# Token shifts folded into doubled weights in a four-layer kernel on one core

## The reference, cut to what matters

```python
xa = _ln(x, ln1_w, ln1_b)
sx = concat([state[:, 1:2] - xa[:, :1], xa[:, :-1] - xa[:, 1:]], axis=1)   # token shift
xxx = tanh((xa + sx * maa_x) @ maa_w1).reshape(b, l, 5, 32)               # mixing network
xxx = einsum('blfd,fde->blfe', xxx, maa_w2)
xm = xa[:, :, None] + sx[:, :, None] * (maa_stack + xxx)                  # five mixed inputs
...                                                                       # w, r, k, v, g and the scan
og = ((og - m) / sqrt(va + 1e-05)).reshape(b, l, e) * gn_w + gn_b
x1 = x + og * g @ Wo.T
xc = _ln(x1, ln2_w, ln2_b)
sx2 = concat([state[:, 0:1] - xc[:, :1], xc[:, :-1] - xc[:, 1:]], axis=1)  # token shift
rr = sigmoid((xc + sx2 * ffn_maa_r) @ Wfr.T)
kk = square(relu((xc + sx2 * ffn_maa_k) @ Wfk.T))
return x1 + rr * (kk @ Wfv.T)
```

## Time and profile before

| | us |
|---|---|
| median of 3 runs (lowest, highest) | 2241.07 (2231.89, 2241.25) |
| the profiled execution | 2240.95 |
| its span, first to last instruction | 2239.2 |
| TensorE, VectorE busy | 1800.2, 1363.9 |
| ScalarE, GpSimd busy | 849.3, 860.1 |

### The profile page before, as it was taken

How to read it: one execution, slowest core, us unless ns; L and a number is a source line. 1 busy time by engine, 2 the same in 40 slices (tenths; PEclk the granted TensorE clock), 3 DMA queues, 4 the chain that set the end, 5 groups by cost and what they waited for, 6 DMA issues and landing times. The chain is left out here.

```text
span 2239.2 us, 37086 instructions
## 1 busy us (share of the span) xinstructions
PE 1800.2 (80%) x13613; PEld 1098.1 (49%) x13613; DVE 1363.9 (61%) x2332; ACT 849.3 (38%) x1680; POOL 860.1 (38%) x905
## 2 busy tenths in 40 slices
PE   3888887888788787887888878788887888788765
PEld 2565444654356444554445634465444654456413
DVE  3652568635886368753687446873578645875283
ACT  1443432533425333353333533253432543425202
POOL 3531257302672037511384114830257303752060
PEclk9999998999899898898988989899988999889967
DMA  5000011010210102010020101201011010200030
GB/s 157 1 1 25 7 39 39 2 41 1 48 30 13 29 1 63 15 35 7 15 63 1 34 8 25 53 2 41 1 39 39 2 39 1 63 15 11 1 77 10
DMA packets 73611, 61.24 MB, mean 27 GB/s; under 512 B 38960, under 2 KB 56512, under 8 KB 73408
## 3 DMA queue, kind: packets, MB, share of 16 engines
q1 hardware_dynamic: 49600, 41.70, 8.9%
q10 hardware_dynamic: 23264, 16.85, 2.6%
q0 software_dynamic: 544, 0.03, 0.0%
HBM read 20.28 MB, written 4.19 MB: 11 GB/s over the span
## 5 line engine op out<-in xcount | busy, mean ns | idle before, releaser
L1508 POOL TENSOR_TENSOR soft_ring<-soft_ring,seg_max 128x512 f32<-128x512 f32 x256 | 324.2, 1274 | 471.7 <-DVE seg_max L1349 470.9
L1056 ACT ACTIVATE soft_ring<-soft_ring 128x512 f32<-128x512 f32 x256 | 160.8, 628 | 399.3 <-POOL soft_ring L1508 391.6
L658 PE MATMUL bank<-late,pick 128*128 128x512 f32 x256 | 176.4, 779 | 97.4 <-DVE late L1197 97.1
L1343 DVE SCALAR_TENSOR_TENSOR soft_ring<-bank,mask 128x512 f32<-128x512 f32 x256 | 164.4, 683 | 108.2 <-PE bank L716 100.4
L1470 POOL TENSOR_TENSOR late<-late 128x520 f32<-128x520 f32 x128 | 188.7, 1474 | 64.8 <-DMA late<-late 50.1
L1185 DVE TENSOR_TENSOR_SCAN late<-late 128x520 f32<-128x520 f32 x128 | 188.3, 1471 | 19.2 <-POOL late L1472 13.7
L857 PEld LDWEIGHTS bank<-ident,soft_ring 128*128 128x128 f32 x1024 | 126.5, 151 | 122.8 <-issue 97.8
L857 PE MATMUL bank<-ident,soft_ring 128*128 128x128 f32 x1024 | 170.0, 298 | 19.8 <-ACTq L1067 14.0
L1516 POOL TENSOR_SCALAR soft_ring<-soft_ring,rden 128x256 f32<-128x256 f32 x64 | 59.1, 924 | 312.4 <-DVE rden L1310 312.4
L716 PE MATMUL bank<-early 64*128 64x512 f32 (+1 forms) x512 | 128.2, 603 | 58.6 <-ACTq L1049 55.2
L1349 DVE TENSOR_REDUCE seg_max<-soft_ring 128x8 f32<-128x512 f32 (+1 forms) x256 | 169.3, 676 | 8.9 <-DVE early L1406 1.9
(11 more groups left out here) (242 smaller groups left out, 3430.1 us busy)
## 6 DMA issues: line engine op xcount, KB each, us to landing
late<-late SPq DMA_DIRECT2D x128, 260.0 KB, 3.0
c<-in_ctx ACTq DMA_DIRECT2D x8, 512.0 KB, 4.3
x<-in_x ACTq DMA_DIRECT2D x8, 512.0 KB, 5.9
out_x<-late SPq DMA_DIRECT2D x8, 512.0 KB, 5.0
mask<-in_mask_Bx1xSxS_ff ACTq DMA_DIRECT2D x16, 128.0 KB, 4.6
w<-in_L_xattn_mlp_w ACTq DMA_DIRECT2D x2, 1024.0 KB
mask<-in_mask_BxS_ik SPq DMA_DIRECT2D x8, 256.0 KB, 4.1
wkv<-in_L_xattn_kv_w ACTq DMA_DIRECT2D x1, 512.0 KB
```

The costliest lines, as they stand in the source:

```text
L658: mm(t[:, :], pick[:, j, :], rs[:, j % 2, :], start=j == 0, stop=j == HS - 1).then_inc(full if j == HS - 1 else sig("rs_used"), 1)
L1056: af(soft[:, u % SOFT, :], soft[:, u % SOFT, :], ACT.Exp).then_inc(sig("exp"), 1)
L1343: stt(out=cuts(u, soft[:, u % SOFT, :]), in0=cuts(u, t[:, :]), scalar=HD1 ** -0.5 if u < UNITS else 1.0 / HD2, in1=mask.unsqueeze(1).broad ...
L1508: tt(s, s, seg_max[:, u % SOFT, 0:segs].unsqueeze(2).broadcast_to([128, segs, 512 // segs]), ALU.subtract).then_inc(sig("sub"), 1)
```

## The change

Both token shifts are written as sums: (x + (prev - x) * m) @ W = x @ (W - mW) + prev @ (mW), with mW the weights scaled row by row. The setup makes `wback` (for `Wfk` and `Wfr`) and `maa1_back`, the scaled weights, and subtracts them from the originals. "maa", "ffn k" and "ffn r" then run twice as many products, on `xcP` or `xaP` at offset 1 and 0. "shift 2" leaves the list of stages, with its entry in `PACE`, so that "ffn k", "ffn r" and "ffn v" fall on steps 58, 60 and 62 (`i` = 54, 56 and 58). "shift" makes `sx` alone. "ffn r" splits its token tile into two halves of 64. `maa2` shrinks to two slabs without zeros, and the mix products contract over 32 rows. The gate uses two operations in place of three. The setup's weight copies wait for their own end.

```diff
-        maa2 = sb("maa2", [128, NMIX, E])
+        maa2 = sb("maa2", [128, 2, E])
...
+        maa1_back = sb("maa1_back", [128, KT, NMIX * DM])
+        wback = {w: sb(f"b_{w}", [128, KT, E]) for w in ("Wfk", "Wfr")}
...
-                for t in (maa2, td2, vbd, pick, ones2):
+                for t in (td2, vbd, pick, ones2):
...
-                    nc.vector.tensor_copy(wt[w][:, :, :].rearrange("p k n -> p (k n)"), t[:, :]).then_inc(free, 1)
+                    link(nc.vector.tensor_copy(wt[w][:, :, :].rearrange("p k n -> p (k n)"), t[:, :]))
+                    dve.sem_inc(free, 1)
...
+                for w, f in (("Wfk", "ffn_k"), ("Wfr", "ffn_r")):
+                    for k in range(KT):
+                        ins = nc.vector.tensor_scalar(wback[w][:, k, :], wt[w][:, k, :], v(f, k), None, ALU.mult)
+                for k in range(KT):
+                    ins = nc.vector.tensor_scalar(maa1_back[:, k, :], maa1[:, k, :], v("maa_x", k), None, ALU.mult)
+                link(ins)
+                nc.vector.tensor_tensor(maa1[:, :, :], maa1[:, :, :], maa1_back[:, :, :], ALU.subtract)
+                for w in wback:
+                    nc.vector.tensor_tensor(wt[w][:, :, :], wt[w][:, :, :], wback[w][:, :, :], ALU.subtract)
...
-                  ["center", "variance", "gate", "project", "moments 2", "normalize 2", "turn 2", "shift 2", "ffn k", "ffn r", "ffn v"])
+                  ["center", "variance", "gate", "project", "moments 2", "normalize 2", "turn 2", "ffn k", "ffn r", "ffn v"])
...
-        PACE = {"r u k": 2.2, "shift": 2.2, "maa": 2.2, "gate": 2.4, "shift 2": 2.2,
+        PACE = {"r u k": 2.2, "shift": 2.2, "maa": 2.2, "gate": 2.4,
...
-                                product((stage, m), 512, [(maa2[:, f, 128 * m:128 * m + 128], xf[:, f // 4, :])], "late")
+                                product((stage, m), 512, [(maa2[rows, f // 4, 128 * m:128 * m + 128], xf[rows, f // 4, :])], "late")
...
-                            pe.wait_ge(sig("x1m_ready"), KT)
-                            product("maaA", 512, [(maa1[:, k, 0:128], xm[:, 0, k, :]) for k in range(KT)], "late")
-                            product("maaB", 512, [(maa1[:, k, 128:160], xm[:, 0, k, :]) for k in range(KT)], "late")
+                            pe.wait_ge(sig("edge3_ready"), 1)
+                            pe.wait_ge(sig("xaP_ready"), KT)
+                            for tile, cols in (("maaA", slice(0, 128)), ("maaB", slice(128, 160))):
+                                product(tile, 512, [(w[:, k, cols], xaP[:, k, :, at:at + L])
+                                                    for w, at in ((maa1, 1), (maa1_back, 0)) for k in range(KT)], "late")
...
-                            pe.wait_ge(sig("xk2_ready"), KT)
-                            square("Wfk", lambda k: xk2[:, k, :])
+                            pe.wait_ge(sig("edge4_ready"), 1)
+                            pe.wait_ge(sig("xcP_ready"), KT)
+                            for m in range(KT):
+                                product((stage, m), 512, [(w["Wfk"][:, k, 128 * m:128 * m + 128], xcP[:, k, :, at:at + L])
+                                                          for w, at in ((wt, 1), (wback, 0)) for k in range(KT)], "late")
...
-                            pe.wait_ge(sig("xr2_ready"), KT)
-                            project("Wfr", xr2)
+                            for q in range(2):
+                                t, full = fill(pe, "late", (stage, q))
+                                for p in range(2):
+                                    terms = [(w, at, k) for w, at in ((wt, 1), (wback, 0)) for k in range(KT)]
+                                    for n, (w, at, k) in enumerate(terms):
+                                        for b in range(2):
+                                            ins = mm(t[64 * b:64 * b + 64, E * p:E * p + E], xcP[:, k, 4 * q + 2 * p + b, at:at + L], w["Wfr"][:, k, :],
+                                                     start=n == 0, stop=n == len(terms) - 1)
+                                ins.then_inc(full, 1)
...
-                                s = batches(sx[:, k, :])
-                                link(tt(s, xaP[:, k, :, 0:L], xaP[:, k, :, 1:LP], ALU.subtract))
-                                stt(out=batches(xm[:, 0, k, :]), in0=s, scalar=v("maa_x", k), in1=xaP[:, k, :, 1:LP],
-                                    op0=ALU.mult, op1=ALU.add).then_inc(sig("x1m_ready"), 1)
+                                ins = tt(batches(sx[:, k, :]), xaP[:, k, :, 0:L], xaP[:, k, :, 1:LP], ALU.subtract)
+                            link(ins)
...
-                                link(tt(ogT[:, k, :], ogT[:, k, :], rgn[:, k, :], ALU.mult))
-                                link(ts(ogT[:, k, :], ogT[:, k, :], v("gn_w", k), v("gn_b", k), ALU.mult, ALU.add))
-                                tt(ogT[:, k, :], ogT[:, k, :], gg[:, k, :], ALU.mult).then_inc(sig("ogT_ready"), 1)
+                                link(stt(out=ogT[:, k, :], in0=ogT[:, k, :], scalar=v("gn_w", k), in1=rgn[:, k, :], op0=ALU.mult, op1=ALU.mult))
+                                stt(out=ogT[:, k, :], in0=ogT[:, k, :], scalar=v("gn_b", k), in1=gg[:, k, :],
+                                    op0=ALU.add, op1=ALU.mult).then_inc(sig("ogT_ready"), 1)
...
-                        elif stage == "shift 2":
-                            dve.wait_ge(sig("edge4_ready"), 1)
-                            for k in range(KT):
-                                dve.wait_ge(sig("xcP_ready"), k + 1)
-                                s = batches(sx2[:, k, :])
-                                link(tt(s, xcP[:, k, :, 0:L], xcP[:, k, :, 1:LP], ALU.subtract))
-                                for dst, name in ((xk2, "k"), (xr2, "r")):
-                                    stt(out=batches(dst[:, k, :]), in0=s, scalar=v(f"ffn_{name}", k), in1=xcP[:, k, :, 1:LP],
-                                        op0=ALU.mult, op1=ALU.add).then_inc(sig(f"x{name}2_ready"), 1)
```

More of the change, by code:

```diff
@@ L244, in build @@
         xcP = cut(late, 0, KT, NB, LP)
-        sx2 = cut(late, 1040, KT, TOK)
-        xk2 = cut(late, 5168, KT, TOK)
-        xr2 = cut(late, 6192, KT, TOK)
         kkT = cut(late, 7216, KT, TOK)
@@ L394, in _ @@
                                 2 * j + k][:, 2 * s:2 * s + 2, :]).then_inc(sig("plain_in"), 16)
-                act.dma_start(maa2[:, 0, :][0:32], a["L3_xattn_maa_w2"][0]).then_inc(sig("plain_in"), 16)
-                for f in range(1, NMIX):
+                for f in range(NMIX):
                     r = 32 * (f % 4)
-                    act.dma_start(maa2[r:r + 32, f, :], a["L3_xattn_maa_w2"][f]).then_inc(sig("plain_in"), 16)
+                    act.dma_start(maa2[r:r + 32, f // 4, :], a["L3_xattn_maa_w2"][f]).then_inc(sig("plain_in"), 16)
                 act.dma_start(td2[64:64 + DD, :], a["L3_xattn_td_w2"]).then_inc(sig("plain_in"), 16)
@@ L601, in mix @@
                         def mix(f):
+                            rows = slice(32 * (f % 4), 32 * (f % 4) + 32)
                             for m in range(KT):
-                                product((stage, m), 512, [(maa2[:, f, 128 * m:128 * m + 128], xf[:, f // 4, :])], "late")
+                                product((stage, m), 512, [(maa2[rows, f // 4, 128 * m:128 * m + 128], xf[rows, f // 4, :])], "late")
                         def square(w, moving):
```

## The result

| | before | after |
|---|---|---|
| median (lowest, highest), 4 runs each on one chip | 2240.73 (2231.89, 2241.25) | 2359.41 (2352.89, 2367.57) |
| ratio to before, 95% interval | | 1.0541 [1.0499, 1.0584] |
| the profiled execution; its span | 2240.95; 2239.2 | 2367.57; 2365.8 |
| mean granted clock of TensorE | 0.907 | 0.895 |

The profiled execution of after is the slowest of its four, so the two traces differ by 126.6 us and the medians by 118.7.

A forecast was written before the change was run, and what follows sets the result against it. TensorE (80% busy) was taken to bound the tail by its own queue, VectorE to be on the head's path. Seven middle blocks at 15.5 (108.7), setup 3.6 and last block 4.2 gave +116.5: 2357 us, range 2305 to 2390.

The forecast's parts named there:

- The tail: From the "turn 2" drains to the MLP in a middle block: added passes and new order start the MLP 11.4 us later.
- last block: Block with layer 3 alone: +4.2 us, of which "ffn r" +3.4; "shift 2" removed against added "ffn k" passes, 0.
- Clock behind the tail: After the last project's chain, 4.6 us of TensorE idle brings slow passes: +2.1 us a middle block.
- Gate: Ahead of the Wo projection: fewer VectorE instructions shorten TensorE's wait, -1.05 us a middle block.
- Head: Start of a middle block: scores start 1.3 us earlier, doubled "maa" takes 3.4 more, +2.1 us.
- Mix products: Mix stages of a middle block: 32-row passes gain nothing, changes of array shape cost +1.0 us.
- Setup: Ahead of the first block: added VectorE work and waiting weight copies, less the removed memset, +3.6 us.
- B: Rival: the tail costs only its added passes, "ffn v" fills another wait, the clock stays; 2312 us, chance 0.18.
- C: Rival: column halves of "ffn r" run one after the other, 7.0 us more in each of 8 blocks; 2413, chance 0.06.
- D: Rival: each change of array shape also lays bare its weight load, 0.36 us a switch; 2378 us, chance 0.08.
- E: Rival, faster: VectorE's time decides and added passes vanish in TensorE's idle 20%; 2192 us, chance 0.05.

The follow-up runs named there:

- first experiment: Changed kernel with "turn 2": 3.8 added to PACE, so the three feed-forward stages stand at old steps 61, 62 and 64: 2299.89 us, ratio to before 1.0295.
- second: Kernel before with "shift 2" at 0.0 in PACE, so the feed-forward stages come at 58, 60 and 62, single weights kept: 2316.84 us, 1.036.

## Why the prediction was right, step by step

The forecast was +116.5 us; the medians differ by 118.7, the traces by 126.6. The tail with the clock behind it was to be 95 of it and is 101 in the traces, so the main path was right. That the total came so near is partly luck: over seven blocks the head was put 10.5 us too high and the mix stages 8.8 too low, and with the last block (6.2 too low) and the tail (5.5 too low) the traces end 10 above the sum.

**The tail (+11.4 a block; measured +12.19).** Right in mechanism and order. Three of the seven tails of after take 46.4 us, 11.5 more than the usual 34.96 of before, and four take 47.9 to 48.0. The 1.6 between them is one thing that the sum lacked: "ffn k" now follows "turn 2" directly, and where TensorE was at the lower clock there, its first four passes take 3.55 us and not 1.96. The rows of the second middle block, then TensorE's windows ahead of "ffn k" and over its first passes, in the first and in the second middle block:

```profile
722.23 1.12 PE L783 MATMUL bank<-ident,c 128*128 128x128 f32 x4 [1.19 <-DVE c L1396]
...
727.06 3.55 PE L589 MATMUL bank<-late,t_Wfk 128*128 128x512 f32 x4 [1.15 <-ACTq L966]
```

```profile
436.00:440.80 4.80, 3.46 (x16) 0.64 0.00 0
441.86:443.65 1.79, 1.79 (x5) 1.00 0.00 0
721.20:726.00 4.80, 3.68 (x16) 0.50 0.00 0
727.06:730.50 3.44, 3.44 (x5) 0.53 0.00 0
```

The same 3.5 to 3.6 us stands in the third, fourth and seventh block, 1.95 or 1.96 in the others. The prediction's parts stand too: the order is worth 7.8 a block with the clock behind it (first experiment), the passes 6.6, and order alone is enough for +3.6% (second).

**Clock behind the tail (+2.1; measured +2.24).** Right: 4.35 us of idle, slow transposes, and 16.08 us of MLP against 13.84. With the stages at their old steps it is 13.84 again.

**Gate (-1.05; measured -0.92 in place).** Right in size where it was looked for. That the gate alone would gain 15 us, twice its own size, was not seen.

**Head (+2.1; measured +0.60).** The mechanism was right, the size was not. Of the +0.60, the part that the change touches, from layer 0's first scores to its first transposes, is +0.80 (14.99 against 14.19 us); the start of the block, unchanged, gives -0.21. The timeline of the first middle block:

```profile
238.21 1.58 PE L737 MATMUL bank<-early 64*128 64x256 f32 x8 [3.96 <-ACTq L1070]
239.72 3.18 PE L589 MATMUL bank<-late,maa 128*128 128x512 f32 x4
```

The scores start 1.47 us earlier than in the earlier trace rows (1.3 was forecast) and take 1.58 us instead of 2.08, behind 3.96 us of idle instead of 5.41. Both kernels stand at the same time there (their first scores start at 233.14 and 233.11), so the clock readings can be compared. "maa" takes 3.18 us for its first four passes (3.4 was forecast) and full speed for the other twelve. It ends at 248.10 against 246.99, +1.1 in this block. The forecast left out that the scores would be quicker (0.5), put the earlier start at 1.3 instead of 1.47, and "maa" at 3.4 more, where it is 3.1. The measured +0.60 lies between the bounds of -0.6 and 2.1, of which the upper was taken.

**Mix products (+1.0; measured +2.26 in the full change, +0.96 alone) and last block (+4.2; measured +10.4).** This is the step that failed, though it moves the sum little: some 9 us over the middle blocks and 5 in the last. The 32-row form was priced by its passes and its switches of shape. The rows bear out the passes: a pass is still 0.43 us where the clock is full. They did not tell that the form itself brings the lower clock. In the last block, where the mix stages follow each other with nothing else on TensorE, it is 5.2 to 5.5 us over the same 60 records (36.18 against 31.03, 36.45 against 30.94), and the full change takes 36.15 us there. (In the first experiment, which also has the 32-row form, it is 33.93.) In a middle block it is 2.66 between the two kernels that differ by it with the new gate and "maa", and 0.96 alone. The remaining 4.9 of the last block lie behind the Wo projection, where 3.4 was forecast: the Wo products themselves take 6.72 us and not 5.78, at the lower clock for longer; the sum had put a gain of clock there. The timeline of after, last block:

```profile
2230.66 3.67 PE L589 MATMUL bank<-late,td 128*64 128x512 f32 x4
...
2243.08 3.60 PE L589 MATMUL bank<-late,t_Wv 128*128 128x512 f32 x8
2246.60 1.98 PE L589 MATMUL bank<-late,maa 32*128 32x512 f32 x4
...
2252.20 5.58 PE L589 MATMUL bank<-late,t_Wr 128*128 128x512 f32 x8
```

The Trainium skill, TensorE: Matmul & The Clock Gate, section Why this matters for your kernels, says that a single K=32 matmul takes the same time as one of K=128, and the full-clock rows agree. It names idle gaps as what brings the lower clock; these rows differ, since the gaps ahead of the fall (0.80 us and 0.2 to 0.3) are the same with 128 rows, where the clock stays full, and the measurement decides. Whether it is the rows in use or another property of the form is not settled; 64 rows lie between.

**Setup (+3.6; measured +4.3 at the start of block 1).** Near. But block 1, whose code is the same, ran 2.6 us shorter, so block 2 starts only 1.7 later.

**The rivals.** B (2312, only the added passes) fell: the stages did take the new order, and what B describes is nearly the first experiment, 2300, which has the old one. C (halves one after the other) fell with 0.110 us a pass. D (0.36 us a switch, for the bared weight load) fell on the rows above: eight passes from 2243.08 at 0.427 end at 2246.50, and the 32-row form starts at 2246.60, a switch of 0.10, as the 0.11 of the earlier trace rows. The period did come out near D's, and the 32-row form costs (268.71 - 266.25) = 2.46 us a block in one pair of kernels that differ by it, but the windows shown with it put that to the clock, in the middle blocks as in the last. E fell with TensorE's busy time, +126 us, and a rise of 5%: in the tail VectorE was not what ended the waits. The busy time of TensorE was forecast at +80. Taken in windows of 2 us, with each one's busy time weighed by its granted clock, 90 of the 126 is work at full clock and 36 the lower clock.

**What stays open.** In stages whose code is unchanged the time moves by 0.4 to 2.6 us with the kernel (head, mix, the first block), by which the clock returns sooner or later. The block start shown under the gate is one such place. What sets the phase of the clock there was not found. The full kernel with mixes over 128 rows was not run.

## What to carry to other kernels

Ask first which engine ends the wait. In the tail it was TensorE's own queue, and turning elementwise work into matmuls lengthened it by 6.6 us a block. In the head it was VectorE in part, and there the same exchange was about even (0.9985, with no change inside its interval). A stage that leaves a list written out by hand moves all that follow: here half of the loss (55 of 119 us) goes when three stages stand where they stood, around one product with a serial chain behind it. A product that fills a serial chain is worth its own length and the clock behind the gap that it covers.

## What the runs showed of the hardware that was not expected

- With products over 32 of 128 rows TensorE's granted clock fell where with 128 it did not, after the same work and the same gaps: over the same 60 records of the last block 0.81 in three kernels and 0.90 in a fourth (32 rows), 0.90 (64 rows), 1.00 in six (128 rows). Cost: 5.2 to 5.5 us in that block, and 2.9 where the clock was 0.90; on the whole 0.9% in one pair of kernels that differ by it, 0.2% in the other.
- Stages whose code is unchanged moved by up to 1.3 us a block with where the clock came back. A change that should save 8 us gained 15, and two changes of 0.15% (not clear of noise) and 0.68% gain gave none together.
- 256-column products with 64 columns of weights, issued in alternation to the two halves of the output's rows, run in pairs: 0.110 us each, against 0.22 for 128 columns.
